# Cross-attention in pairs of images, with row-tiled transposed scores and one exponential for an image

## The reference

```
q = layernorm(x) @ q_w + q_b;  k, v = ctx @ kv_w + kv_b          # 16 heads of 8
attn = softmax(q k^T / sqrt(8));  x1 = x + (attn v) @ proj_w + proj_b
xn = layernorm(layernorm(x1)) * gamma + beta;  w, idx = top2(softmax(xn @ router_w^T / 1.5))
out = x1 + layernorm(x1) + sum over the 2 experts of w * (silu(xn @ W1[e]) @ W2[e])
```

## Time and profile before

| | |
|---|---|
| runs shown | 843.8, 844.96, 849.12 us; median 844.96 |
| profiled execution | 845.43 us; span of its trace 843.5 us, so 1.9 us lie around it |
| busy in the span | PE 721.3, PEld 496.7, DVE 543.0, ACT 499.3, POOL 492.0 us |
| mean granted clock of TensorE | 0.926 of 2.4 GHz |
| attention phase | to about 511 us; experts from there to 843 |

### The profile page before, as it was taken

The page is one execution under the profiler, slowest core; times in us unless marked ns, Lnnn a source line. Parts: engine busy times, 40 slices in busy tenths (PEclk is TensorE's granted clock), DMA queues, the critical chain, the costliest instruction groups (busy, mean ns, idle before and its releaser), DMA issues. The chain is left out here.

```text
span 843.5 us, 16697 instructions
## 1 busy us (share of the span) xinstructions
PE 721.3 (86%) x5164; PEld 496.7 (59%) x5164; DVE 543.0 (64%) x1857; ACT 499.3 (59%) x1037; POOL 492.0 (58%) x692
## 2 busy tenths in 40 slices
PE   1699999998989899998999977988899889999960
PEld 1455556555656555564665545766677677777840
DVE  1456666765776667675666734666677777688972
ACT  1366666565566566564666544856675766677840
POOL 5422526657566747665765560664577777765772
PEclk9699989988999989998999965989999999999995
DMA  5455454554565537455442434655987875779964
GB/s 180 110 115 135 113 135 115 161 122 130 118 159 145 139 81 186 101 158 121 105 105 67 100 107 167 202 192 192 318 301 241 290 214 185 254 246 366 377 214 179
DMA packets 152287, 146.49 MB, mean 174 GB/s; under 512 B 53403, under 2 KB 108584, under 8 KB 152040
## 3 DMA queue, kind: packets, MB, share of 16 engines
q1 hardware_dynamic: 140808, 121.57, 50.0%
q0 software_dynamic: 9088, 19.68, 6.8%
q10 hardware_dynamic: 2304, 4.20, 1.3%
HBM read 81.56 MB, written 40.86 MB: 145 GB/s over the span
## 5 line engine op out<-in xcount | busy, mean ns | idle before, releaser
L837 ACT ACTIVATE P<-pt 77x512 f32<-77x512 f32 x256 | 151.5, 593 | 117.3 <-PE pt L641 108.8
L1350 POOL DMA_INDIRECT ys<-yo,to x156 | 167.6, 1074 | 75.2 <-issue 39.6
L1343 POOL DMA_INDIRECT xs<-zz,idx x128 | 131.1, 1024 | 94.8 <-PE pt L563 35.3
L973 DVE TENSOR_REDUCE mx<-ps 128x4 f32<-128x308 f32 x256 | 118.8, 471 | 88.4 <-PE ps L628 84.3
L1213 DVE TENSOR_TENSOR sl<-sf,sh 128x512 fp32r<-128x512 f32 x156 | 107.2, 691 | 63.6 <-ACT sh L884 28.3
L641 PE MATMUL pt<-qd,kc 128*77 128x512 f32 x256 | 115.2, 451 | 15.6 <-DMA qd<-nm 14.9
L652 PE MATMUL po<-P,v 77*9 77x128 f32 x2048 | 107.2, 284 | 4.8 <-ACT osb L845 4.5
L628 PE MATMUL ps<-kd,qc 128*128 128x308 f32 x256 | 107.5, 421 | 1.6 <-DMA kd<-kc 0.9
L882 ACT ACTIVATE sf<-ps 128x512 f32<-128x512 f32 x78 | 46.9, 601 | 68.8 <-PE ps L563 46.6
L641 PEld LDWEIGHTS pt<-qd,kc 128*77 128x77 f32 x256 | 38.9, 152 | 50.5 <-issue 29.1
L628 PEld LDWEIGHTS ps<-kd,qc 128*128 128x128 f32 x256 | 50.6, 198 | 25.9 <-issue 19.9
(11 more groups left out here) (207 smaller groups left out, 1802.7 us busy)
## 6 DMA issues: line engine op xcount, KB each, us to landing
qd<-qc SPq DMA_DIRECT2D x128, 128.0 KB
ws<-wsd SPq DMA_DIRECT2D x26, 512.0 KB
w1o<-wsd SPq DMA_DIRECT2D x26, 512.0 KB
w2o<-wsd SPq DMA_DIRECT2D x26, 512.0 KB
xb<-xs SPq DMA_DIRECT2D x39, 288.0 KB
kd<-kc SPq DMA_DIRECT2D x128, 77.0 KB
wsd<-ws SPq DMA_DIRECT2D x8, 1024.0 KB
y<-ys SPq DMA_DIRECT2D x32, 256.0 KB
```

Source lines behind the costliest of these rows:

```text
L837: eng.activation(P[k % 4][:, :], pT[k % 2][0:CS, :], ACT.Exp, scale=SCALE).then_inc(sems["p"], 1)
L973: eng.tensor_reduce(mx[b % 2][:, 4 * g:4 * g + 4], ps[k % 2][:, 0:KC].rearrange("p (j m) -> p j m", j=4), AX.X, ALU.max, negate=True).then ...
L1343: eng.indirect_dma_start(out=xs, out_offset=at, in_=zz[b][:, j % 4, :], in_offset=None).then_inc(sems[f"sw{b}"], 16)
L1350: eng.indirect_dma_start(out=ys, out_offset=at, in_=yo[u % NYO][:, q, :], in_offset=None).then_inc(sems[f"ys{u % NYO}"], 16)
```

## The change

Images go in pairs p (32 of them), two pairs to a group. `slot` takes the place of SLOTS and `front`: EVEN and ODD are the orders of a group's two pairs, and LATER and SOONER say which pair or group each step works for.

- ST(p, i), one image, is 16 matmuls: four sets g by four row strips j, each on 32 partitions of kc and qc directly, 128 moving columns, each strip into a bank of its own. QD and qd are gone. All four score banks are one tensor pT without a second buffer, and EX(p, i) is one exponential of 77 x 2048.
- nm of a pair (32 x 128) goes into rows 24, 56, 88 and 120 of qc by four DMAs (ND), which ScalarE issues. KD copies 24 rows of each strip, not 32.
- SC has no banks of its own: its scores take turns in pm0 to pm2 (SC is in BANKED).
- PV(p) does a pair in one block of 32 matmuls: v18 holds v in columns 0 to 7 and a one in 8 for the first image, 9 to 16 and 17 for the second, and the two accumulate. po, osb, OT, the division, ON, and PR serve two images at once.
- MT follows SC13 of the same pair at once; PR comes three pairs after.
- The first table of expert blocks covers 16 blocks, not 18, and is made one group earlier; xin has six buffers.

```diff
-K1 = 18
+K1 = 16
...
-N_LDW, N_LDV, N_CV = 6 * 16, 13 * 16, 15
+N_LDW, N_LDV, N_CV = 6 * 16, 13 * 16, 21
 ONE_EPS, EPS_EPS = 1.0 + EPS, EPS * EPS
 
-SLOTS = "SC0 Pv2 ST0 ON SC1 Pv3 ST1 MT SC2 ST2 PR Pu0 OT SC3 ST3 Pu1"
+EVEN = ("ST0 CT XT EX0 SC10 SC11 KP PV SC12 KL SC13 MT QP OE ND QL ON A0 "
+        "ST1 EX1 SC00 KG0 SC01 KG1 OT SC02 KG2 SC03 KG3 PR A1 A2 LX")
+ODD = ("KD0 ST0 EX0 SC10 QG0 SC11 QG1 PV SC12 QG2 SC13 MT QG3 OE ND ON XH VP "
+       "ST1 EX1 SC00 KD1 SC01 OT SC02 XP SC03 PR")
+LATER = {"ST": 1, "EX": 1, "PV": 2, "OE": 2, "OT": 2, "ON": 3, "PR": 3, "MT": 0, "ND": 0, "SC1": 0, "SC0": -1}
+SOONER = {"CT": 1, "XT": 1, "KP": 1, "KL": 1, "QP": 1, "QL": 1, "KG": 1, "QG": 1, "VP": 1, "A0": 2, "A1": 2, "A2": 2, "XH": 2, "XP": 2, "LX": 3}
...
+    def slot(s):
+        k, odd = divmod(s, 2)
+        steps = []
+        for name in (ODD if odd else EVEN).split():
+            stem, digits = name.rstrip("0123456789"), [int(d) for d in name if d.isdigit()]
+            if stem == "A":
+                steps += at(k + 2, name)
+            elif stem == "KD":
+                steps += [("KD", 2 * k + 2 + digits[0])] if 0 <= k + 1 < NC else [None]
+            elif stem in SOONER:
+                c = k + SOONER[stem]
+                steps += [(stem, c, *digits)] if 0 <= c < NC else [None]
+            else:
+                p = s - LATER[name[:3] if stem == "SC" else stem]
+                steps += [(stem, p, *digits)] if 0 <= p < NP else []
+        return steps
...
+        return ([("PD",)] if c == NC - 1 else []) + [("TN", i, j) for j in range(3)] + {NC - 5: table(1), NC - 1: table(2)}.get(c, [])
...
+    def routed(c):
+        turned = tails[0].index(("ZT", c)) if ("ZT", c) in tails[0] else -4
+        tails[1].extend(gap(max(turned + 4 - len(tails[1]), 0)) + router(c))
+
+    ok = lambda p: 0 <= p < NP
+    for s in range(-6, NP + 4):
+        k, odd = divmod(s, 2)
+        if odd and 0 <= k - 2 < NC - 1:
+            tails[0] += norms(k - 2)
+        if odd and 0 <= k - 3 < NC - 2:
+            routed(k - 3)
+        if s >= 2 and s % 3 == 2 and s // 3 < E:
+            put(("WL", s // 3))
+        if s >= 4 and s % 3 in (1, 2) and (s - 4) // 3 < E:
+            put(("WS", (s - 4) // 3, s % 3 - 1))
+        for step in slot(s):
+            put(step)
...
-COUNTED = (7, 11, 12, 15)
-BANKED = ("XT", "QP", "CT", "KP", "QG", "KG", "VP", "MT", "OT", "ON", "PR", "ZT", "RT", "RK", "TM")
+COUNTED = (7, 10, 11, 15)
+BANKED = ("SC", "XT", "QP", "CT", "KP", "QG", "KG", "VP", "MT", "OT", "ON", "PR", "ZT", "RT", "RK", "TM")
...
+NX = 6
...
-        qd = tile(sa, "qd", [128, 2, 4, 4, S], R, 2)
...
+        v18 = tile(sa, "v18", [CS, 2, 2, H, 18], F, 2)
+        P = tile(sa, "P", [CS, 4, 4, S], F, 4)
+        mx = tile(sa, "mx", [128, 32], F, 2)
+        nm = tile(sa, "nm", [32, 128], R, 2)
...
-        pm, ps, pT, po = pt("pm", 3), pt("ps", 2), pt("pt", 2), pt("po", 1)[0]
+        pm, po = pt("pm", 3), pt("po", 1)[0]
+        pT = st.enter_context(nc.psum_tensor("pt", [128, 4, 512], F))
...
+                    load(kd[s][32 * j:32 * j + 24, :, :, j, :].rearrange("p i g m -> p (i g) m").bitcast(F),
+                         kc[c % 2][32 * j:32 * j + 24, i:i + 2, :, :].rearrange("p i g m -> p (i g) m").bitcast(F), f"kd{s}")
...
+            def SC(p, i, g):
+                c, n_ = p // 2, 2 * (p % 2) + i
                 w.wait_ge(*qc_done(c, g))
                 w.wait_ge(f"kd{p % 2}", 64 * (p // 2 + 1))
+                t, s, n = bank("SC", p, i, g)
+                w.wait_ge(s, n)
+                eng.matmul(t[:, 0:KC], qc[c % 2][:, n_, g, :], kd[p % 2][:, i, g, :, :], start=True,
                            stop=True).then_inc(sems["S"], 1)
 
+            def MT(p):
+                w.wait_ge(*freed("SC", p, 1, 3))
+                t, s, n = bank("MT", p)
+                w.wait_ge(s, n)
+                eng.transpose(t[0:32, 0:128], mx[p % 2][:, :], idf[:, :]).then_inc(sems["mT"], 1)
+
+            def ST(p, i):
+                c, n_ = p // 2, 2 * (p % 2) + i
+                w.wait_ge(f"nm{p % 2}", 64 * (p // 2 + 1))
+                w.wait_ge("p", 2 * p + i)
+                for g in range(4):
+                    for j in range(4):
+                        at_j = slice(32 * j, 32 * j + 32)
+                        ins = eng.matmul(pT[0:CS, j, g * S:(g + 1) * S], kc[c % 2][at_j, n_, g, :], qc[c % 2][at_j, n_, g, :],
+                                         start=True, stop=True)
+                ins.then_inc(sems["T"], 1)
+
+            def PV(p):
+                c = p // 2
                 w.wait_ge(*freed("VP", c))
                 w.wait_ge("c_v", N_CV)
+                w.wait_ge("p", 2 * p + 2)
+                w.wait_ge("osb", p)
+                for g in range(4):
+                    for i in range(2):
+                        for j in range(4):
+                            ins = eng.matmul(po[32 * j:32 * j + 18, g * 128:(g + 1) * 128], v18[c % 2][:, p % 2, i, 4 * g + j, :],
+                                             P[(2 * p + i) % 4][:, j, g, :], start=(i == 0), stop=(i == 1))
                 ins.then_inc(sems["Og"], 1)
...
-                    w.wait_ge("S", 16 * (c - 1))
-                    for p in (2 * c - 4, 2 * c - 3):
-                        w.wait_ge(f"qd{p % 2}", 64 * (p // 2 + 1))
+                    w.wait_ge("T", 4 * (c - 1))
...
+            def MT(p):
+                t, s, _ = bank("MT", p)
+                w.wait_ge("mT", p + 1)
+                if p >= 2:
+                    w.wait_ge(f"nm{p % 2}", 64 * (p // 2))
+                eng.copy(nm[p % 2][:, :], t[0:32, 0:128]).then_inc(sems[s], 1)
+
+            def ND(p):
+                c, i = p // 2, 2 * (p % 2)
+                w.wait_ge(*freed("MT", p))
+                for j in range(4):
+                    eng.dma_start(qc[c % 2][32 * j + 24:32 * j + 25, i:i + 2, :, :].rearrange("p i g n -> p (i g) n").bitcast(F),
+                                  nm[p % 2][8 * j:8 * j + 8, :].bitcast(F)).then_inc(sems[f"nm{p % 2}"], 16)
+
+            def EX(p, i):
+                w.wait_ge("T", 2 * p + i + 1)
+                w.wait_ge("Og", p - 1)
+                eng.activation(P[(2 * p + i) % 4][:, :, :, :], pT[0:CS, :, :].rearrange("m j (g n) -> m j g n", g=4), ACT.Exp,
+                               scale=SCALE).then_inc(sems["p"], 1)
+
+            def OE(p):
+                w.wait_ge("Og", p + 1)
+                w.wait_ge("oX", p - 1)
                 w.wait_ge("c_v", N_CV)
+                eng.copy(osb[p % 2][:, :, :], po[:, :]).then_inc(sems["osb"], 1)
+
+            def ON(p):
+                t, s, _ = bank("ON", p)
+                w.wait_ge("onT", p + 1)
+                w.wait_ge("pr", p - 1)
+                eng.copy(oT[p % 2][:, :, :], t[:, 0:256].rearrange("p (i d) -> p i d", i=2)).then_inc(sems[s], 1)
...
+                v = t[0:CS, :].rearrange("p (u i h d) -> p u i h d", u=2, i=2, h=H)
+                b = vbb[:, :].rearrange("p (h d) -> p h d", h=H).unsqueeze(1).to_broadcast([CS, 2, H, 8])
+                eng.tensor_tensor(v18[c % 2][:, :, 0, :, 0:8], v[:, :, 0, :, :], b, ALU.add)
+                eng.tensor_tensor(v18[c % 2][:, :, 1, :, 9:17], v[:, :, 1, :, :], b, ALU.add).then_inc(sems[s], 1)
+
+            def SC(p, i, g):
+                t, s, _ = bank("SC", p, i, g)
+                w.wait_ge("S", 8 * p + 4 * i + g + 1)
+                w.wait_ge("mT", p - 1)
+                eng.tensor_reduce(mx[p % 2][:, 4 * i + g:32:8], t[:, 0:KC].rearrange("p (j m) -> p j m", j=4),
+                                  AX.X, ALU.max, negate=True).then_inc(sems[s], 1)
```

More of the change, by code:

```diff
@@ L63, in stage_order @@
     at = lambda c, *names: [(n, c) for n in names] if 0 <= c < NC else []
[L64 to L76, removed]
+    gap = lambda n: [None] * int(n)
+    def slot(s):
[14 more added lines that the diff above has]
+        return steps
     def norms(c):
@@ L117, in go @@
             put(steps.pop(0) if steps else None)
[L119 to L149, removed]
-            go()
-        for step in near[fed:]:
-            put(step)
-    tails[1] += gap(max(len(tails[0]) - len(tails[1]), 0) + 3) + router(NC - 2)
+    def routed(c):
[14 more added lines that the diff above has]
+            put(step)
+            go()
+    routed(NC - 2)
     tails[0] += norms(NC - 1)
-    tails[1] += gap(max(len(tails[0]) - len(tails[1]), 0) + 5) + router(NC - 1)
+    routed(NC - 1)
     blocks = True
@@ L381, in xattn_moe @@
         flat = lambda t: t[:, :, :].rearrange("p a b -> p (a b)")
-        hid = ps + pT
+        hid = [pT[:, k, :] for k in range(4)]
         W2v = W2.rearrange("e (k p) d -> e p k d", p=128)
@@ L526, in YL @@
                 w.wait_ge(f"so{k}", 16 * (c // 4))
-                last = K1 + 7 if c < 8 else K1 + 12 if c < 12 else NBLK - 1
+                last = K1 + 7 if c < 8 else K1 + 14 if c < 11 else NBLK - 1
                 for s in range(NYO):
@@ L646, in PV @@
+            def PV(p):
+                c = p // 2
```

(27 more changed lines are left out.)

193 lines of the change are left out of this document (55 added, 138 removed).

## The result

The changed kernel takes 1020.9 us (median of 4 runs, 1020.0 to 1024.0) against 844.4: 1.209 times as long, 95% interval [1.203, 1.216]. The forecast, 871 us with a range of 785 to 905, had the sign and a sixth of the size.

A forecast was written before the change was run, and what follows sets the result against it. TensorE's order of work was taken as the bound, plus DMA waits and half-clock stretches. Groups: 28.4 us replayed plus 3.0 for the clock, 31.4 against 29.8; 16 groups +26, phase ends +1, giving 871 us, range 785 to 905.

The forecast's parts named there:

- I take 0.25 of the time, a mean clock of 0.87: TensorE in the attention phase: low clock for a quarter of the time, adding 3.0 us a group.
- rival 3: Attention phase: clock low half the time, 34.4 us a group, 918 us; chance 0.08.
- 20 x 0.6 = 12 us: TensorE, attention: extra time of a group wholly at 1.2 GHz, from work taking 1.6 times as long.
- the replay's 28.4: Attention group followed in written order, waits included: 28.4 us at full clock.
- ScalarE's issues: ND's four DMA issues, ahead of ON's copy on ScalarE: 1.35 to 2.25 us, delaying SC01 and EX1.
- EX: ScalarE's exponential of 2048 columns: 1.95 us, holding up whatever stands behind it.
- The waits by place: TensorE waiting at MT, KG0, SC01, OT, RK, SC03 and PR: 7.05 us a group.
- No standing waits for nm: TensorE's waits for the DMA of negated maxima count as gone, with some 4 us from issue to use.
- PV's block: TensorE: 16 separate PV blocks a group become two of 8 x 0.22 + 0.12 us, saving 1.6 us.
- ST's block: Row-tiled ST on TensorE: 0.7 us an image, saving 0.9 us a group; wrong if outside 0.5 to 1.1 us.
- The expert phase: The part after attention: the same instructions, so no change in time.
- the clock term: TensorE in attention: falls to the lower clock add 3.0 us a group, making 31.4 us.

The follow-up runs named there:

- e9: The changed kernel run a second time, nothing altered: 1025 us, 1.212 times the kernel before.
- m2: Not the computation: TensorE patterns alone, blocks separated by waits for a ScalarE copy; PV blocks with 0.74 us waits stayed at the lower clock for the 120 us.
- e6: The changed kernel with the order of e3 and ND's four DMAs issued by SP, not ScalarE: 921 us against 846, ratio 1.09.
- m1: Not the computation: TensorE patterns alone, meant without waits, each after 100 full-array matmuls; PV and the mixture held 2.4 GHz.
- e3: The changed kernel with only its order mended (KL ahead of SC12, MT later, EX1 behind KG1): 948 us, ratio 1.169 to the kernel before.
- e15: The changed kernel with order mended, ND by SP, PV on 128 rows, and full-array matmuls of constants where TensorE waits: 1.045 times the kernel before.
- m3: Not the computation: TensorE patterns with waits of about 0.7 us, varying rows, columns and tiling; 77-row PV and row-tiled ST fell, 128-row column-tiled sets held.
- e16: The kernel before with one added wait an image for VectorE's maximum and PV on 128 rows: 1.102 times the kernel before.

## Why the prediction was wrong

**What failed is one step: "I take 0.25 of the time, a mean clock of 0.87".** Measured: 0.84 of the time (0.76 in e9), a clock of 0.58 to 0.62. Even rival 3 had only half. I reasoned from single waits in the kernel before, each followed by 6.6 us at the lower level, and took a fall in the changed kernel to be as short. It isn't: 11 of its 13 low stretches last 17 to 48 us, and the clock comes back between them mostly for less than 4 us. In m2 a PV pattern with waits fell once and never came back for as long as it ran.

What keeps the clock down is shown in part. PV on 77 rows is one cause: padding it shortened the falls and gave 39 to 46 us. The waits are another: mending order and issue (e6) brought the ratio from 1.21 to 1.09, though this also takes away the waits' own time. That ST and OT, being cut, left too little work between the waits is my guess; no run tried it.

**Its price was mis-sized** as well: "20 x 0.6 = 12 us" for a group wholly at the lower clock. The factor 1.6 came from a short PV block with its change of layout. From start to start a whole PV block goes from 1.87 us (m1) to 3.54, 1.9 times; a score from 0.24 to 0.42, nearly 1.8; ST from 0.43 to 0.71, 1.65. With the measured share and the old price 28.4 + 0.84 x 12 is 38.5; the group takes 42.4, so the price was nearer 17 than 12, an estimate that takes the replay's 28.4 as right.

**ScalarE's issues**: bounded at 1.35 to 2.25 us for four; they are 0.63 each, 2.6 us. The row of out<-y, one contiguous store, was the wrong neighbour; SP's nm copy at 0.56 was the same kind of copy and nearer. Given to SP, with the order mended, they were worth 0.08 (e3 to e6, on two kinds of chip, one run of e6).

**What held.** EX: 1.88 for 1.95. The waits by place in 350 us: MT for the maxima 17.8 us, OT for kc 13.3, SC01 for oT 11.5; 6.8 us a group in all, for 7.05. No standing waits for nm: one of 2.7 us in all. PV's block: 1.87 for 1.88. ST's block was cheaper than forecast, 0.43 us up to the next start at the upper clock, which by the prediction's own sign (0.5 to 1.1) is a miss; the change of layout on the way in isn't in that distance. The expert phase was the same within 5 us. The sign hung on the clock term alone, since 28.4 by itself is below the 29.8 of before; that term had the right direction and a fifth of its size, 3.0 for 14.0 us a group.

**What stays open.** With order, issue, rows and most waits mended, e15 is still 4.5% behind at clock 0.82, and none of its groups with the router in it ran wholly at 1.00. Row-tiled ST fell in m3 as well, and how much of the rest hangs on it wasn't tried. Nor did I find why chips differ by 4% on the kernel before; about half of it lies in the expert phase, which took 308 to 317 us in the profiles from the faster chips and 329 to 337 in the others.

## What to carry to other kernels

Before taking work off a TensorE that is busy 90%, read what the clock does behind its waits, and how long it stays down: lighter work with waits cost more here than it saved, and a busy share read at the lower clock doesn't show it. Try matmuls with a short contraction on all 128 rows over zeros: here it cost no matmul time and gave 0.75% on a tuned kernel and about 4% on the changed one, and in one kernel (e16) nothing. DMA issues on a computing engine are work of that engine: four in a row held ScalarE for 2.6 us.
